# One-hot tiles of the guard in a graph attention kernel: 16-bit operands, eight chunks innermost, transposed from a strided view

## The reference, cut to what matters

```python
def _attention_aggregate(h_proj, sender, receiver, attn_vec, num_nodes):
    h_sender = h_proj[sender]
    h_receiver = h_proj[receiver]
    e = jnp.einsum('ehd,hd->eh', h_sender, attn_vec[:, :HD]) + jnp.einsum('ehd,hd->eh', h_receiver, attn_vec[:, HD:])
    e = jax.nn.leaky_relu(e, NEG_SLOPE)
    e_max = jax.ops.segment_max(e, receiver, num_segments=num_nodes)
    alpha = jnp.exp(e - e_max[receiver])
    alpha_sum = jax.ops.segment_sum(alpha, receiver, num_segments=num_nodes)
    alpha = alpha / (alpha_sum[receiver] + EPS_SOFTMAX)
    msg = h_sender * alpha[..., None]
    return jax.ops.segment_sum(msg, receiver, num_segments=num_nodes)
h_in = _attention_aggregate(h_proj, src, dst, a_in, n)
h_out = _attention_aggregate(h_proj, dst, src, a_out, n)
```

## Time and profile before

| | us |
|---|---|
| median of three runs | 3366.75 |
| lowest and highest of them | 3361.63, 3368.27 |
| the profiled execution: its own time | 3377.51 |
| its span, first to last instruction | 3375.7 |
| busy: TensorE matmul | 2190.7 |
| busy: TensorE weight load | 1296.6 |
| busy: VectorE | 2277.1 |
| busy: ScalarE | 835.0 |
| busy: GpSimd | 1657.2 |

### The profile page before, as it was taken

One profiled execution on the slowest core, in us unless ns is written; L12 is line 12 of the kernel. 1 busy time (PEld: TensorE's weight loads), 2 busy tenths in 40 slices (PEclk: granted clock), 3 DMA queues, 4 the chain that ended last, 5 costly groups with the idle time before them and its releaser, 6 DMA issues.

```text
span 3375.7 us, 46741 instructions
## 1 busy us (share of the span) xinstructions
PE 2190.7 (65%) x12603; PEld 1296.6 (38%) x12659; DVE 2277.1 (67%) x3122; ACT 835.0 (25%) x1389; POOL 1657.2 (49%) x1455
## 2 busy tenths in 40 slices
PE   0488877777895989994963444434566665528562
PEld 0233455554452455542442111111456611118562
DVE  8999888898549720055132544444986799979777
ACT  0099433332001110022000111111344322206341
POOL 7400133332057777777104777777876777710000
PEclk9799999999997999997975555565569999955897
DMA  2000011110443524400725434435358733530452
GB/s 71 0 0 0 30 44 44 44 44 34 159 124 98 147 65 99 84 1 1 170 45 97 115 111 111 117 110 108 85 165 264 233 111 110 98 33 0 150 177 74
DMA packets 195115, 301.52 MB, mean 89 GB/s; under 512 B 120540, under 2 KB 133818, under 8 KB 194922
## 3 DMA queue, kind: packets, MB, share of 16 engines
q1 hardware_dynamic: 138986, 175.88, 16.7%
q0 software_dynamic: 40512, 62.87, 10.8%
q10 hardware_dynamic: 15552, 61.94, 6.0%
HBM read 191.65 MB, written 88.01 MB: 83 GB/s over the span
## 4 chain that ended last, share of the span: by engine, by line
PE 35%; POOL 19%; DVE 17%; issue 17%; DMA 6%; ACT 5%; ACTq 1%; DVEq 0%; SPq 0%; POOLq 0%; PEldq 0%
POOL arena L1304 19%; PE PS L537 11%; PE PS L698 9%; PE PS L883 6%; DMA arena<-T_att,idx 5%; ACT arena L513 4%; DVE arena L558 4%; PE PS L972 3%; PE PS L475 2%; PE PS L959 1%; DVE arena L1195 1%; DVE arena L373 1%; DVE arena L489 1%; DVE arena L566 1%; DMA T_att<-parts 1%
## 5 line engine op out<-in xcount | busy, mean ns | idle before, releaser
L1304 POOL DMA_INDIRECT arena<-T_att,idx x864 | 845.9, 979 | 323.1 <-issue 229.1
L537 PE MATMUL PS<-arena 128*128 128x400 f16 (+2 forms) x4320 | 780.6, 332 | 270.4 <-issue 112.1
L1139 DVE TENSOR_REDUCE arena<-PS 128x1024 f32 (+1 forms) x432 | 502.6, 1212 | 334.3 <-PE PS L1106 334.0
L537 PEld LDWEIGHTS PS<-arena 128*128 128x128 f16 (+2 forms) x4320 | 528.2, 158 | 513.6 <-issue 350.9
L1477 POOL DMA_INDIRECT order<-arena x400 | 514.2, 1285 | 249.4 <-issue 249.4
L558 DVE TENSOR_SCALAR arena<-arena 128x1600 f16<-128x1600 f16 x448 | 392.3, 919 | 63.1 <-PE PS L537 59.0
L1106 PE MATMUL PS<-arena,pick 128*128 128x512 bf16 x812 | 319.1, 493 | 154.1 <-DVE arena L1139 140.2
L698 PE MATMUL PS<-arena 128*128 128x512 f16 (+1 forms) x1575 | 318.1, 361 | 95.4 <-issue 82.1
L632 POOL TENSOR_TENSOR rdeg<-rdeg,arena 128x1600 f32<-128x1600 f32 x48 | 160.7, 3348 | 311.8 <-ACT arena L616 311.8
L1095 PE MATMUL PS<-ident_b,score_buf 128*32 128x128 bf16 x864 | 90.4, 268 | 314.8 <-ACT score_buf L1068 305.2
L698 PEld LDWEIGHTS PS<-arena 128*128 128x128 bf16 x1575 | 147.9, 99 | 261.6 <-issue 110.2
(11 more groups left out here) (258 smaller groups left out, 2781.0 us busy)
## 6 DMA issues: line engine op xcount, KB each, us to landing
spill<-arena SPq DMA_DIRECT2D x108, 560.0 KB, 2.9
arena<-spill ACTq DMA_DIRECT2D x108, 560.0 KB, 3.8
arena<-A SPq DMA_DIRECT2D x50, 800.0 KB, 4.6
A<-arena SPq DMA_DIRECT2D x50, 400.0 KB, 2.4
arena<-A SPq DMA_DIRECT2D x50, 400.0 KB, 3.3
arena<-T_att,idx POOLq DMA_INDIRECT x864, 2.6
order<-arena POOLq DMA_INDIRECT x400
T_att<-h SPq DMA_DIRECT2D x2, 1600.0 KB, 13.9
```

What stands on the lines that cost most here:

```text
L537: return t.matmul(where, lhsT, rhs, start=False, stop=True, skip_group_check=True)
L1139: v.tensor_reduce(cmax[d][:, u:u + 2, bass.ds(i * SLOTS + half * GROUP + q // 2 * QUAD, QUAD)], PS[:, u * BANK:(u + 2) * BANK].rearrange(" ...
L1304: p.indirect_dma_start(out=ring1[:, b, j, :], out_offset=None, in_=T_att[d][:, :], in_offset=bass.IndirectOffsetOnAxis(ap=idx[:, d, k:k + ...
```

## The change

The comparison's two inputs become bf16 in SBUF: `steps_8` holds each step number eight times in a row, and `key_16` the keys. Both are written at the head of `guard_dve` in each direction, in the place of `sT`, which only the top uses. The group in `eq` is now laid out with the eight chunks innermost: `eq[e, j]` in place of `eq[j, e]`. TensorE's transposition of chunk j therefore loads a weight tile whose columns lie eight numbers (16 bytes) apart. The values are the same: all numbers from -1 to 127 are exact in bf16. `steps_at` stays in PSUM for the weighted stage.

```diff
-        eq = OH_flat.bitcast(BF16).rearrange("p (g j e) -> p g j e", g=LAP, j=GROUP)
+        eq = OH_flat.bitcast(BF16).rearrange("p (g e j) -> p g e j", g=LAP, j=GROUP)
+        steps_8 = view(23104, GROUP * P // 2).bitcast(BF16).rearrange("p (e j) -> p e j", j=GROUP)
+        key_16 = view(23104 + GROUP * P // 2, CHUNKS // 2).bitcast(BF16)
...
         def guard_dve(v, d):
 
 
+            v.tensor_copy(steps_8, iota[:, 0:P].unsqueeze(2).to_broadcast([P, P, GROUP]))
+            v.tensor_copy(key_16[:, 0:CH[d]], key[:, d, 0:CH[d]])
             ct = chunk_tile[:, d, 0:CH[d]]
...
                 c = bass.ds((i * LAP + b) * GROUP, GROUP)
-                v.tensor_tensor(eq[:, b % LAP, :, :], steps_at.unsqueeze(1).to_broadcast([P, GROUP, P]),
-                                key[:, d, c].unsqueeze(2).to_broadcast([P, GROUP, P]), ALU.is_equal) \
+                v.tensor_tensor(eq[:, b % LAP, :, :], steps_8, key_16[:, c].unsqueeze(1).to_broadcast([P, P, GROUP]),
+                                ALU.is_equal) \
                     .then_inc(oh_again, 1)
...
                 for j in range(GROUP):
-                    last = t.transpose(bank[:, j * P:(j + 1) * P], eq[:, b % LAP, j, :], ident_b[:, :])
+                    last = t.transpose(bank[:, j * P:(j + 1) * P], eq[:, b % LAP, :, j], ident_b[:, :])
```

## The result

| | kernel before | with the change |
|---|---|---|
| median, us | 3365.64 | 3370.61 |
| lowest and highest, us | 3359.54, 3369.15 | 3364.98, 3374.50 |
| executions | 20 | 20 |

The ratio is 1.0015, with a 95% interval of 1.0008 to 1.0021. That is 5.0 us slower, inside the 0.2% that the prediction called no change. The prediction had +1.4 us and 3368.0.

The account below looks back on a forecast made before the run. VectorE was taken to pace the second guard, which starts 11.3 us after GpSimd's last cast. A gain of 8.6 us there and 10 us lost by GpSimd gave 3366.75 + 1.4 = 3368 us; 8-in-10 range 3357 to 3382.

Parts of the forecast that it names:

- Part 1: VectorE's comparison in the guard loops: falls from 1.22 us to 0.69 us with 16-bit inputs in SBUF.
- Part 2: Second guard's loop: TensorE becomes the bound, 1.35 us per plain group, 1.82 with the branch, a lap 5.87 for 6.53 us.
- Part 3: TensorE's strided weight loads in the guard: 166 against 151 ns at half clock, mostly hidden, 0.02 us per group.
- Rival (b): TensorE's transpositions: the strided load is not hidden, making the kernel slower, 3381 to 3414 us; chance 0.15 for +7 us or more.
- Part 4: Head of the second guard: the two added casts are not hidden and cost 1.0 us, at worst 1.6.
- The second guard's sum: Second guard: 8.6 us from 13 shorter laps, 1.0 from faster filling, less 1.0 for casts; gain 8.6 us.
- Part 5: First guard's loop: VectorE's comparison holds GpSimd to one gather each, delaying the last cast and second guard by 10 us.
- The sum: Whole kernel: -8.6 us in the second guard and +10 us from GpSimd's delay make +1.4 us, 3368 us.
- The markers: Trace signs: comparison 0.69 us, second loop 80 us, gathers 1.1 to 1.3, last cast at 2993, L1068's waits some 60.
- Rival (a): GpSimd's gathers aren't held, or their loss is made up later: only the second guard's -8.6 us, 3358; chance 0.15.
- (c): Guard loops: TensorE's clock rises, 1.32 us per group, 1.44 with the branch; -2 to -4 us, 3363 to 3365; chance 0.15.
- (d): Guard comparison stays at 1.22 us despite 16-bit inputs, GpSimd held and losing 18 us: 3386 us; chance 0.04.

Follow-up runs that it names:

- the memsets: Kernel before with ten memsets of 128 x 768 on GpSimd ahead of groups 54 to 63 of the gathers: 3379.41 us, ratio 1.0036.

## Why the prediction was right, and where its sizes were off

**Part 1** held: 681 ns, predicted 690.

**Part 2** named the right bound. The three plain groups of a lap are 1.36 to 1.42 us where I had 1.35 for each, the one with the branch 1.85 where I had 1.82. The lap of the earlier trace rows was predicted at 5.87 us and is 6.01. The takes start 0.84 us after the turns, as before; it is the step from the takes to the next turns that is 0.52 to 0.59 us rather than 0.52. Thirteen laps give 13 x 0.52 = 6.8 us, and the faster fill 0.5 us where I had 1.0. The loop gains 88.55 - 81.28 = 7.3 us, not 9.6: that term was mis-sized by a quarter, within its bounds.

**Part 3** held: loads of 165 ns at the median in the second loop for the predicted 166, and no cost in the pace. The pace shows that the stream of the transposition before hides them. The Trainium skill (SBUF — State Buffer, Door 1: The DMA port swizzle, on cachelines) says that each access that crosses to a new 16-byte line pays a penalty. The runs agree, with 17 ns for a load of 128 columns. Rival (b) is refuted at this clock.

**Part 4**: the two casts start at 2995.66 and the guard's first old instruction at 2996.58, so 0.9 us for the predicted 1.0.

**The second guard's sum**: 7.3 - 0.9 = 6.4 us where 8.6 was predicted. From the last cast to the start of the loop's last comparison it is 133.2 us in the profile of the change and 138.5 us in that of before, 5.3 us less. Of the missing 1.1 us, 1.0 lies in the top's last maxima: from GpSimd's last cast to VectorE's next stage it is 12.3 us with the change (2983.39 to 2995.66), 12.7 in the kernel with the second direction only, and 11.3 before. Nothing was changed there. The two casts behind it are not the reason, since the kernel with the fp32 comparison from SBUF has none in its second guard and takes 11.9 us (2990.95 to 3002.88). What these three share is a lower granted clock of TensorE behind the last cast. Before, then with the change (us, busy shares, clock as in the earlier trace rows), and VectorE's maxima with the change:

```profile
2983.20:2987.00 3.80, 2.42 (x15) 0.79 (x14) 3.77 (x4) 2.08 (x3) 0.16 (x1) 1.00 0.38 151
2983.50:2987.00 3.50, 3.40 (x14) 1.29 (x14) 3.06 (x6) 2.17 (x3) 0.16 (x1) 0.50 0.42 164
2986.60 9.14 DVE L1141 TENSOR_REDUCE arena<-PS 128x8 f32<-128x1024 f32 x8 [0.44 <-PE PS L1108]
```

At the lower clock VectorE waits 0.44 us for TensorE's masks (0.50 and 0.57 in the two others), a wait that the profile of before doesn't have. The rest, 0.1 to 1.0 us, is how far VectorE has got with its maxima when the last cast comes: in the kernel with the first direction only the clock is 1.00 there and it is 11.8 us all the same. Why the clock stood lower in three of the six traces from chips with some 3370 us isn't settled. The run with the second direction only, at -7.1 us (-4.7 to -10.8 by its interval), agrees with either number.

**Part 5** held in its mechanism, and within the loop in its size. It said one gather per comparison, and there are 51 in 51 steps; a median of 1.1 to 1.3 us, and it is 1.165; a gather's end 0.83 us behind the comparison's, and that is what the rows show. The loss was put at 10.2 us, and gather by gather the loop costs 10.4. What the prediction didn't have is how much the way from the loop to the last cast differs between executions. By the trace of the change 9.5 us are left in the last cast, by that with the first direction only 14.6, and its time is 12.7 us longer (7.7 to 16.2 by its interval).

The Trainium skill (SBUF — State Buffer, Who interferes with whom) says that a `tensor_tensor` was not seen to stall a DMA. The runs show the opposite here, for 16-bit and 32-bit operands alike: a median of 1161 ns for 944 and of 1272 ns for 944, and 12.7 and 16.5 us in the end. The same section says that an operation with two SBUF inputs contends with an instruction of GpSimd that reads SBUF. With that half the runs agree, since a gather takes its indices from SBUF. Which access of the gather it is that waits, no run here tells.

**The sum**: +1.4 us predicted, +5.0 measured. The interval (+2.7 to +7.1) leaves out the +1.4, so something was mis-sized. The gain is: 6.4 us by the trace for 8.6, which explains 2.2 of the 3.6 us. The rest is no more than the loss varies by behind the loop. That the result is so near to zero is no merit of either term: a gain and a loss of 6 to 13 us nearly cancel, and a few us more in one of them would have carried it past the 0.2%.

**The markers.** One of them failed and deserves a note. I had said that the last cast would be at 2993, ten later than at 2983.1, and it is at 2983.39. Likewise the waits of ScalarE's copy (L1070 with the change, L1068 before) from 2930 on are 52.4 us, for the 60 that I expected. Both numbers stood on a position in one profiled execution that was 10.8 us above its median, and 7.8 us of that lay in the very stretch of gathers that I measured from. I had scaled the sum to the median, but not the marker. Rival (a) would have been read out of this, wrongly; the run with the second direction only settled it.

**The rivals.** (a) is refuted as a whole by the kernels with one direction each and by the memsets: GpSimd is held, and its delay reaches the end. A part of its second half is true, since some of the delay can be made up in the weighted stage (4.9 us in the trace of the change). (b) is refuted, above. (c): the granted clock is 0.57 and 0.58 in the loops for 0.50 and 0.53, so it stayed near the half level, and the case did not arise. (d) is refuted by 681 ns. A rival that I did not have is that the gathers are over before the first guard begins. Then both guards gain, and the result is 10 us faster: that is what the chips with 4090 us showed.

**A version that beats the kernel before on both kinds of chip** comes out of it: the change in the second direction only, 0.9977 on the chip with 3368 us and 0.9979 on one with 4090. It beats the whole change only where GpSimd's gathers run beside the first guard. On chips with 4090 us the whole change has 0.9968, which the intervals don't tell from 0.9979.

## What to carry to other kernels

Before a faster form of a VectorE operation goes in, look at what runs on GpSimd beside it: an input in PSUM may be what keeps GpSimd free, and moving it to SBUF can cost more than the faster form gains. Use the new form where GpSimd has nothing to do beside it, or where nothing waits for GpSimd. When a marker is a position in a trace, take it from a kernel that shares the stretch ahead of it, count it from the head of that stretch, and don't take it from one execution that stood apart from its median.

## What I had not expected of the hardware

The same program took 3368 us on one chip and 4090 on two others, and there it stands still in the first direction's top in waits named "remote" (888.7 us on ScalarE, up to 43.7 at once). The gathers are over before the first guard begins there, and with that the same change has opposite signs: 1.0015 and 0.9968. Why the top stands still stays open.

The hold seems to work in the other direction too, though slightly. In the first guard's loop, beside GpSimd, a comparison takes up to 800 ns, in the second at most 696:

```profile
L1199 DVE TENSOR_TENSOR arena<-arena x52: 677/682/800, 2401.9 to 2476.7; 128x1024 bf16<-128x1024 bf16 x52
```

Eight of the 52 take more than 0.70 us. Seven of them are the ones beside GpSimd's seven casts, and the eighth starts within 0.02 us of a gather. The trace with the first direction only shows the same: eight above 0.70 us, seven of them beside its seven casts. No experiment was made on it. One of them, of 0.76 us, starts at 2436.81, 0.08 us after a cast of GpSimd does:

```profile
2436.73 0.28 POOL L1317 CAST W<-arena 128x96 bf16<-128x96 f32 x1
...
2436.81 0.76 DVE L1199 TENSOR_TENSOR arena<-arena 128x1024 bf16<-128x1024 bf16 x1
```

It seems that a cast of GpSimd can be held like a gather. In the kernel with the fp32 comparison from SBUF six of the seven casts in the loop take 0.85 to 0.87 us where it is 0.27 or 0.28 otherwise. The one below ends at 2431.35, just behind the end of VectorE's comparison (2430.01 + 1.22 = 2431.23):

```profile
2430.48 0.87 POOL L1314 CAST W<-arena 128x96 bf16<-128x96 f32 x1
```
